# Row sums of a softmax over partitions: transposes and a sum over columns in place of products with a column of ones

## The reference

```python
memory_proj = einsum('bme,de->bmd', memory, W_mem)
scores = einsum('bnd,bmd->bnm', hidden_states, memory_proj) / sqrt(D)
attn = softmax(scores, axis=-1)
memory_context = einsum('bnm,bmd->bnd', attn, memory_proj)
gate_input = concatenate([hidden_states, memory_context], axis=-1)
gate = sigmoid(einsum('bnf,df->bnd', gate_input, W_gate) + b_gate)
fused = hidden_states + gate * memory_context
return fused * rsqrt(mean(square(fused), axis=-1) + 1e-6) * norm_w
```

## Time and profile before

| | us |
|---|---|
| runs | 561.5, 561.4, 561.13 |
| median of the runs | 561.4 |
| the profiled execution | 562.44 |
| its span, first to last instruction | 560.6 |
| PE busy in it | 541.7 |
| DVE busy | 503.4 |
| ACT busy | 336.2 |
| POOL busy | 134.1 |

### The profile page before, as it was taken

One profiled execution on the slowest core, in us unless ns is written; L12 is line 12 of the kernel. 1 busy time (PEld: TensorE's weight loads), 2 busy tenths in 40 slices (PEclk: granted clock), 3 DMA queues, 4 the chain that ended last, 5 costly groups with the idle time before them and its releaser, 6 DMA issues.

```text
span 560.6 us, 9004 instructions
## 1 busy us (share of the span) xinstructions
PE 541.7 (97%) x2432; PEld 438.8 (78%) x2432; DVE 503.4 (90%) x847; ACT 336.2 (60%) x633; POOL 134.1 (24%) x102
## 2 busy tenths in 40 slices
PE   8999999999999999999999999999999999999992
PEld 7777888878887788878888788887888778887871
DVE  4879959999899998899998998999988999889966
ACT  4676646665567646576366665666565864667534
POOL 0005600244003520055001440025300451005600
PEclk9999999999999999999999999999999999999988
DMA  9965371520683117711385115841088212100033
GB/s 226 260 127 83 90 132 50 98 73 18 148 176 97 37 50 136 167 68 37 98 163 104 56 37 134 171 114 40 0 170 177 75 37 99 52 23 20 0 114 112
DMA packets 184338, 54.25 MB, mean 97 GB/s; under 512 B 161528, under 2 KB 174848, under 8 KB 184320
## 3 DMA queue, kind: packets, MB, share of 16 engines
q1 hardware_dynamic: 183792, 53.52, 40.9%
q10 hardware_dynamic: 528, 0.52, 0.3%
HBM read 45.63 MB, written 8.39 MB: 96 GB/s over the span
## 4 chain that ended last, share of the span: by engine, by line
PE 66%; DVE 17%; issue 10%; SPq 3%; ACT 2%; DMA 2%; ACTq 0%; DVEq 0%
PE bank L357 14%; PE bank L358 13%; PE bank L359 13%; PE bank L524 7%; PE bank L525 7%; PE bank L526 7%; DVE p_lo L838 5%; DVE s L879 3%; DVE fused L984 2%; DVE fused L991 2%; DVE gate L905 2%; ACT fused L696 2%; DVE gate L934 2%; DMA fused<-in_L_xattn_W_gate_dram 2%; SPq L249 2%
## 5 line engine op out<-in xcount | busy, mean ns | idle before, releaser
L1155 POOL TENSOR_TENSOR psum_rows<-psum_rows,p_tmp 128x512 f32<-128x512 f32 (+1 forms) x88 | 122.5, 1392 | 85.4 <-ACT p_tmp L673 84.3
L838 DVE TENSOR_TENSOR p_lo<-p_tmp,p_hi 128x512 fp32r<-128x512 f32 (+1 forms) x104 | 92.3, 889 | 5.5 <-ACT p_hi L635 5.4
L673 ACT ACTIVATE p_tmp<-s 128x512 f32<-128x512 f32 (+1 forms) x104 | 65.2, 628 | 45.1 <-DVE s L879 44.5
L1155 POOL TENSOR_TENSOR psum_rows<-p_tmp 128x512 f32<-128x512 f32 x8 | 10.8, 1354 | 309.4 <-ACT p_tmp L673 309.4
L357 PE MATMUL bank<-q_hi,mt_hi 128*128 128x512 f32 (+1 forms) x208 | 81.7, 393 | 0.0
L358 PE MATMUL bank<-q_lo,mt_hi 128*128 128x512 f32 (+1 forms) x208 | 81.2, 390 | 0.0
L359 PE MATMUL bank<-q_hi,mt_lo 128*128 128x512 f32 (+1 forms) x208 | 81.1, 390 | 0.0
L525 PE MATMUL bank<-p_lo,mem_hi 128*128 128x512 f32 (+1 forms) x208 | 81.0, 389 | 0.0
L524 PE MATMUL bank<-p_hi,mem_hi 128*128 128x512 f32 (+1 forms) x208 | 81.0, 389 | 0.0
L526 PE MATMUL bank<-p_hi,mem_lo 128*128 128x512 f32 (+1 forms) x208 | 80.9, 389 | 0.0
L635 ACT ACTIVATE s<-bank 128x512 f32<-128x512 f32 (+1 forms) x104 | 62.0, 597 | 19.5 <-PE bank L359 19.1
(11 more groups left out here) (93 smaller groups left out, 1057.6 us busy)
## 6 DMA issues: line engine op xcount, KB each, us to landing
mem_raw<-in_ctx_dram SPq DMA_DIRECT2D x48, 256.0 KB, 3.0
mem_blocks<-in_ctx_dram SPq DMA_DIRECT2D x64, 136.0 KB
x_again<-in_x_dram SPq DMA_DIRECT2D x32, 256.0 KB, 2.6
out_dram<-fused SPq DMA_DIRECT2D x32, 256.0 KB, 2.1
x_raw<-in_x_dram SPq DMA_DIRECT2D x112, 64.0 KB, 2.1
mem_blocks<-in_ctx_dram SPq DMA_DIRECT2D x56, 64.0 KB, 2.0
x_raw<-in_x_dram SPq DMA_DIRECT2D x4, 256.0 KB, 4.7
gate<-in_L_xattn_W_gate_dram SPq DMA_DIRECT2D x2, 512.0 KB, 6.1
```

Source lines behind the costliest of these rows:

```text
L673: nc.scalar.activation(p_tmp[0:r, t % TMP_RING, :], s[0:r, t, :], ACT.Exp, scale=float(D) ** -0.5).then_inc(exp_done, 1)
L838: return nc.vector.tensor_tensor(dst, src, hi.bitcast(F32), ALU.subtract)
L1155: nc.gpsimd.tensor_tensor(psum_rows[0:r, :], a, p_tmp[0:r, t % TMP_RING, :], ALU.add).then_inc(p_added, 1)
```

## The change

`row_sums` no longer multiplies by a column of ones. Four PE transposes turn the groups of `psum_rows` over, into all 512 columns of bank 3; then DVE adds over the columns of each group into a new tile `row_sum`, 128 x 4 in SBUF, and the reciprocal reads that tile behind a semaphore of its own, `sum_done`. The column `ones`, its memset and its wait are gone.

```diff
-        ones = sb("ones", [P, 1])
+        row_sum = sb("row_sum", [P, NT])
...
-        cleared, ready_ident, ready_ones, ready_pad = (
-            sem("cleared"), sem("ready_ident"), sem("ready_ones"), sem("ready_pad"))
+        cleared, ready_ident, ready_pad = sem("cleared"), sem("ready_ident"), sem("ready_pad")
...
-        p_added = sem("p_added")
+        p_added, sum_done = sem("p_added"), sem("sum_done")
...
                 for j in range(NT):
-                    last = nc.tensor.matmul(bank[MAX_BANK][:, j : j + 1], psum_rows[:, j * P : (j + 1) * P],
-                                            ones[:, :], start=True, stop=True)
+                    last = nc.tensor.transpose(
+                        bank[MAX_BANK][:, j * P : (j + 1) * P], psum_rows[:, j * P : (j + 1) * P], ident[:, :])
                 last.then_inc(pe_sum, 1)
...
             pe.wait_ge(ready_ident, 1)
-            pe.wait_ge(ready_ones, 1)
             transpose_first_x()
...
                 dve.wait_ge(pe_sum, b + 1)
-                nc.vector.reciprocal(r_sum[:, :], bank[MAX_BANK][:, 0:NT]).then_inc(r_first, 1)
+                nc.vector.tensor_reduce(row_sum[:, :], bank[MAX_BANK][:, :].rearrange("p (a n) -> p a n", a=NT),
+                                        AX.X, ALU.add).then_inc(sum_done, 1)
+
+                dve.wait_ge(sum_done, b + 1)
+                nc.vector.reciprocal(r_sum[:, :], row_sum[:, :]).then_inc(r_first, 1)
...
-            nc.vector.memset(ones[:, :], 1.0).then_inc(ready_ones, 1)
-
```

## The result

The changed kernel took 565.46 us in the median of 6 runs (564.95 to 566.79), the kernel before 561.45 beside it (6 runs, 561.13 to 562.55). The ratio is 1.0072, 95% interval 1.0056 to 1.0088: 4.0 us slower. The forecast was 566.4 us, range 564.7 to 568.1. Its direction and range held; it was 0.9 us too high. When both were run again, the medians were 566.71 and 562.24, ratio 1.0088 (1.0070 to 1.0107).

A forecast was written before the change was run, and what follows sets the result against it. The loop was taken as bound by DVE's chain from the reciprocal to add_bias, then PE's gate_x(3) and dense PE. Seven times 0.71 us, 5.0 us, with nothing for PE's saving or the ends, gave 566.4 us, range 564.7 to 568.1.

The forecast's parts named there:

- What bounds the kernel: Each iteration: PE's scores, DVE's chain with the reciprocal, PE's gate_x(3), dense PE; row sums lie beside that chain.
- What PE saves: Row sums: four transposes for four products save 0.47 us per iteration, ending in a longer wait, value nothing.
- What DVE pays: In reciprocal(b): a reduce of 0.68 us plus 0.03 for dependence, 0.71 us per iteration.
- The low end: DVE's added sum at independent spacing, 0.60 us per iteration, 4.2 us in all, 565.6 us; 0.08 of the 0.78.
- Does it pass through: From r_sum to gate_x(2) and gate_x(3) everything comes 0.71 us late; seven iterations give 5.0 us.
- The ends of the program: Start and tail: nothing; the tail's reduce is covered, with 0.7 us of cover left.
- its recovery: Rival, chance 0.06: PE's clock in the tail no longer falls to 1.2 GHz, 1.6 us less, 564.8 us.
- PE as bound: Rival, chance 0.04: row sums on the path, 7 x 0.47 = 3.3 us gained, 558.1 us.
- a near tie: At ACT's L696: the ways over PE and DVE nearly tie; tanh on ACT frees it at 299.88.
- The hidden reduce: Rival, chance 0.04: the 0.77 us gap before L984 hides the reduce, 561.4 us, no change.
- Falls of the clock in the loop: Rival, chance 0.08: PE's waits at gate_x and spread_max lower its clock, 1.6 us each, 568.0 to 577.6 us.

The follow-up runs named there:

- the DVE part alone: Kernel before, products with ones kept, plus DVE's sum over columns (unused) and its wait ahead of the reciprocal: period 66.72 us, 566.75 us, ratio 1.0075.
- the PE part alone: Changed kernel without the sum over columns and its wait, the reciprocal reading four transposed columns: period 65.99 us, 560.96 us, ratio 0.9973.
- the kernel without the wait: Kernel before plus DVE's unused sum over columns, without a semaphore between sum and reciprocal: period 66.59 us, 565.65 us.
- the early kernels: mem_lo(3), mem_lo(4) one pair of score tiles earlier: kernel before 561.25 us, changed 561.67; with mem_lo(5) behind the column maxima too: 561.56 and 558.23.

## Why the prediction was right, point by point

**What bounds the kernel.** Confirmed by the two halves: the DVE part alone has the changed kernel's period, the PE part alone the old one. The chain DVE to ACT to DVE up to `add_bias`, and PE's wait behind it, set the loop's period. One reading was off: DVE was last released by PE at 296.41, and not at 295.00, from where the prediction calls it dense. The sum lies behind both, so nothing in the forecast hung on it.

**What PE saves.** 0.47 us, measured 0.47. That it has no value was right for this order of DVE's work only.

**What DVE pays.** The sum takes 677 to 681 ns, median 680, like the maximum. The step to its follower is 0.72 us, 0.71 forecast; the period grew by 0.69 (66.02 to 66.70 or 66.72), and six iterations by 4.12 us, against 7 x 0.71 for all: the term stands at 4.8 (4.12 + 0.66) in place of 5.0. The low end, 0.60 by plain spacing, is what the sum costs without a dependence, as the kernel without the wait shows.

**Does it pass through.** Yes, with the sizes given above. At `spread_max` PE's first load started 0.38 us behind the start of the last matmul ahead of it (303.61 after 303.23), where before the two started together; 0.40 was forecast. At `gate_x(2)` PE's loss was 1.27 us (1.11 + 0.16), 1.13 forecast: behind a wait the four transposes need 0.41 us from the first load to the next matmul (303.61 to 304.02) and not 0.58, so PE was back 0.15 us sooner than I had it. It ended in the wait and changed nothing.

**The ends of the program.** This is the term that was off, by its size. It was put at nothing, with the tail's lower clock carried along as a fixed part of the kernel and its recovery as a rival of 0.06. In the two profiles the tail did shrink by 1.58 us, as that rival had it (1.6), and the median of 565.46 lies between the forecast and the rival's 564.8, nearer to the latter. But the kernel before has the lower mean clock in 28 of 66 runs only, and the changed one in none of 12. The difference of the two kinds' medians, 2.0 us, times 28/66 is 0.8 us, and 4.8 - 0.8 = 4.0 is what the first set measured (the second gave 4.5). The means say the same: the 12 runs of the changed kernel average 566.1 us, 4.9 above the 561.2 of the 38 runs of the kernel before at the higher mean clock and 4.1 above the 562.0 of all 66. That agrees in size, yet the 66 runs are not those of the first set, whose clocks are not on record, and the runs compared come from different sets; the start of the program adds to the uncertainty. There PE waits for `W_gate` between nothing and 1.7 us in the twelve profiles, and the first row sums come between 96.7 and 98.8 us.

**The rivals.** PE as bound (558.1) fell, though the reason against it was too strong: the chain of waits that runs over L459 was not a misreading. The way over PE tied with that over DVE, as the early kernels show. I had called it a near tie and gave ACT's tanh as the holder; in fact each of the two alone holds L696, PE's at + 4.38 and DVE's at + 4.39. Had the sum been free, the gain would still have been nil, which is what the PE part alone shows. The hidden reduce (561.4) fell: the gap moved with the chain. Falls of the clock in the loop did not come: with waits of 1.11 and 0.68 us, the stretches of the changed kernel from 294 to 336 read 1.00.

```profile
308.00:322.00 14.00, 12.21 (x53) 9.49 (x52) 13.76 (x18) 11.10 (x24) 8.22 (x6) 1.00 0.24 72
```

The Trainium skill, "TensorE: Matmul & The Clock Gate", section "Part 4: PE-mode transpose", says that transposes don't count as PE being busy in the same way. No run here measures that by itself. In the loop 12 transposes per iteration left the clock at 1.00, and in the tail the lower mean clock was rarer with them (1 of 52 runs) than with the one-column products (36 of 109).

## What to carry to other kernels

Moving work from the engine with the highest share to the next one is decided at the wait where the two meet, not by their shares: find the last wait of the one for the other, and ask on whose side of it the work lands. Where two ways to one instruction tie, taking from one gives nothing and adding to the other costs in full; reorder the second first, then the saving on the first pays. And take the tail's clock from several runs before it goes into a sum.

## What the runs showed of the hardware

Four fp32 products with one column cost PE more than four 128-column transposes: 8 loads and 8 matmuls, 0.82 us beyond the normal step, against 0.35 (1.05 and 0.58 us from the last score matmul to the next product). Behind 8 such matmuls and a wait of 0.4 us for DVE, PE's clock fell to 0.50 of full speed, 1.2 GHz, in two profiles, and behind the same matmuls and the same wait it stayed at 1.00 in four others. In one and the same kernel the mean clock of 28 runs in 66 suggests such a fall. Between the sum over columns and the reciprocal, a wait on the instruction just ahead costs DVE 0.12 us: 0.72 us from start to start in place of 0.60.
